# GNN with two residual-norm layers: one pick in every layer-0 step, 3.6 per layer-1 iteration, and the comparison numbers read from PSUM

## The reference, cut to what matters

```python
def _L0_gnn_ref(x, edge_index, edge_attr, W1, b1, W2, b2):
    src, dst = (edge_index[0], edge_index[1])
    tmp = jnp.concatenate([x[dst], x[src], edge_attr], axis=1)      # 48 + 48 + 32
    h = jax.nn.relu(tmp @ W1 + b1)                                  # 128
    msg = h @ W2 + b2                                               # 48
    return jax.ops.segment_sum(msg, dst, num_segments=N_NODES)
def _L1_gnn_ref(node_feat, edge_feat, src, dst, eps):
    m = jax.nn.relu(node_feat[src] + edge_feat)
    neigh = jax.ops.segment_sum(m, dst, num_segments=N_NODES)
    return (1.0 + eps[0]) * node_feat + neigh
x = _layernorm(x + _L0_gnn_ref(x, edge_index, edge_attr_32, W1, b1, W2, b2), axis=-1)
x = _layernorm(x + _L1_gnn_ref(x, edge_attr_48, src, dst, eps), axis=-1)
```

## Time and profile before

| | us |
|---|---|
| three runs | 4407.39, 4453.33, 4467.84; median 4453.33 |
| the profiled execution, its own time | 4415.78 |
| its span, first to last instruction | 4413.9 |
| TensorE's granted clock, mean over the span | 0.863 of full speed |
| busy: PE, PEld, VectorE, ScalarE, POOL | 3796.9, 2973.1, 2131.5, 664.9, 2860.8 |

### The profile page before, as it was taken

One profiled execution on the slowest core, in us unless ns is written; L12 is line 12 of the kernel. 1 busy time (PEld: TensorE's weight loads), 2 busy tenths in 40 slices (PEclk: granted clock), 3 DMA queues, 4 the chain that ended last, 5 costly groups with the idle time before them and its releaser, 6 DMA issues.

```text
span 4413.9 us, 56486 instructions
## 1 busy us (share of the span) xinstructions
PE 3796.9 (86%) x21170; PEld 2973.1 (67%) x21170; DVE 2131.5 (48%) x4283; ACT 664.9 (15%) x1275; POOL 2860.8 (65%) x2700
## 2 busy tenths in 40 slices
PE   4678888898999889899997898889689787897988
PEld 2556666676677667677766676668568576675777
DVE  1233333343333334334334576657468565674655
ACT  1212221122122122122221000000000000000111
POOL 6566666666666656656563677767678767676763
PEclk8678998898888888888887898889789998898888
DMA  4122222222222222222221122222122222221221
GB/s 99 28 34 32 33 34 32 32 35 32 34 32 35 32 32 34 32 32 34 35 35 33 41 49 48 46 43 53 39 46 55 45 45 44 43 52 39 50 48 41
DMA packets 407403, 178.33 MB, mean 40 GB/s; under 512 B 279173, under 2 KB 406291, under 8 KB 407027
## 3 DMA queue, kind: packets, MB, share of 16 engines
q0 software_dynamic: 86272, 66.43, 10.8%
q1 hardware_dynamic: 318738, 107.75, 10.7%
q10 hardware_dynamic: 2114, 0.49, 0.1%
HBM read 169.43 MB, written 5.00 MB: 40 GB/s over the span
## 4 chain that ended last, share of the span: by engine, by line
PE 65%; another core or an unknown queue 13%; issue 11%; POOL 5%; DVE 5%; DMA 0%; DVEq 0%; ACT 0%; POOLq 0%; SPq 0%
PE ps_h L830 12%; PE ps_t L830 12%; PE ps_early L830 11%; PE ps_m L740 8%; PE ps_h L791 7%; PE ps_as L732 6%; POOL edge L542 5%; PE ps_t L758 4%; PE ps_nodes L840 2%; PE ps_as L777 2%; DVE picked L1046 1%; DVE edge L957 1%; DVE at_place L1037 1%; DVE acc L971 1%
## 5 line engine op out<-in xcount | busy, mean ns | idle before, releaser
L542 POOL DMA_INDIRECT edge<-x,resid_sb x1438 | 1444.6, 1005 | 884.0 <-issue 405.3
L542 POOL DMA_INDIRECT edge<-x_dram,resid_sb x1258 | 1416.0, 1126 | 621.1 <-issue 381.8
L830 PE MATMUL ps_h<-x_parts,at_place 125*128 125x480 f32 x3080 | 772.7, 401 | 71.6 <-issue 64.1
L830 PE MATMUL ps_t<-x_parts,at_place 125*128 125x480 f32 x3040 | 771.5, 406 | 57.1 <-issue 54.8
L830 PE MATMUL ps_early<-x_parts,at_place 125*128 125x480 f32 x2520 | 706.7, 427 | 94.3 <-DVE edge L957 47.3
L830 PEld LDWEIGHTS ps_h<-x_parts,at_place 125*128 125x128 f32 x3080 | 600.4, 198 | 204.6 <-issue 104.3
L830 PEld LDWEIGHTS ps_t<-x_parts,at_place 125*128 125x128 f32 x3040 | 598.3, 201 | 185.8 <-issue 90.0
L830 PEld LDWEIGHTS ps_early<-x_parts,at_place 125*128 125x128 f32 x2520 | 498.1, 199 | 293.0 <-issue 170.5
L1037 DVE TENSOR_TENSOR at_place<-place_row,places_sb 125x1280 fp32r<-125x1280 f32 x432 | 640.1, 1482 | 1.4 <-DMA place_row<-rows_dram 1.2
L732 PE MATMUL ps_as<-edge,msg 128*48 128x48 f32 x6256 | 367.8, 222 | 219.1 <-issue 173.9
L732 PEld LDWEIGHTS ps_as<-edge,msg 128*48 128x48 f32 x6256 | 300.7, 132 | 330.0 <-issue 261.8
(11 more groups left out here) (63 smaller groups left out, 1769.0 us busy)
## 6 DMA issues: line engine op xcount, KB each, us to landing
e_sb<-e SPq DMA_DIRECT2D x196, 192.0 KB
place_row<-rows_dram SPq DMA_DIRECT2D x432, 62.5 KB
edge<-e SPq DMA_DIRECT2D x196, 128.0 KB
edge<-x,resid_sb POOLq DMA_INDIRECT x1438
edge<-x_dram,resid_sb POOLq DMA_INDIRECT x1258
x_win<-xT SPq DMA_DIRECT2D x391, 9.0 KB
acc<-xT SPq DMA_DIRECT2D x10, 234.4 KB
feats<-x SPq DMA_DIRECT2D x10, 234.4 KB
```

The costliest lines, as they stand in the source:

```text
L542: pool.indirect_dma_start(out=cols, out_offset=None, in_=rows_of, in_offset=bass.IndirectOffsetOnAxis(ap=index, axis=0)).then_inc(done, 16)
L830: last = nc.tensor.matmul(banks[q % len(banks)], lhsT=at_place[:, q % PLACED, c, :], rhs=x1_parts[:, c, part, :], start=(c == 0 and part = ...
```

## The change

- Layer 0: `plan_pairs` puts all ten units of one pick into every step from 19 to 187: 169 picks for 126.
- Layer 0, VectorE: `find_places` is called inside `offset_messages`, ahead of line 974 and behind the wait for the output layer, no longer after it. It is the same pick in the same step.
- Layer 1: the rates are 9 and 8 units in a step for 8 and 7: 345 picks for 306, or 3.6 in an iteration for 3.2 at first. A pick may be found half a step later relative to its first unit (1.5 for 1.9): 154 of the 345 are now found one step before their first unit is multiplied, where all were found two steps before.
- The numbers that `find_places` compares with are copied once to PSUM, behind `ps_m` in its bank, and read there (`ps_places` for `places_sb`). The bank's tensor is now named `ps_out`.

```diff
                 select = math.ceil(end - 0.38)
-                picks.append((select + 1, math.floor(begun - 1.9), select))
+                picks.append((select + 1, math.floor(begun - 1.5), select))
...
-    for s in range(first, last - 2, 4):
-        for begin, end in ((s, s), (s + 1, s + 1), (s + 2, s + 3)):
-            q, each = len(picks), CHUNKS // (end - begin + 1)
-            for step in range(begin, end + 1):
-                units[step] = [(q, (step - begin) * each + c) for c in range(each)]
-            picks.append((2 * (end + 2) + 1, begin - 1, end + 1))
+    for step in range(first, last):
+        units[step] = [(len(picks), c) for c in range(CHUNKS)]
+        picks.append((2 * (step + 2) + 1, step - 1, step + 1))
...
-PLAN, PRODUCTS = plan([(s, 10 if s < 0 else 8 if s < UNROLL * NORM_ITER else 7) for s in range(-AHEAD, GROUPS)], GROUPS - 1)
+PLAN, PRODUCTS = plan([(s, 10 if s < 0 else 9 if s < UNROLL * NORM_ITER else 8) for s in range(-AHEAD, GROUPS)], GROUPS - 1)
...
-        ps_m = pb("ps_m", [P, 2, TILES, D])
-        ps_iota = ps_m[:, 0, 0, 0:WIN]
+        ps_out = pb("ps_out", [P, 2 * TILES * D + CHUNKS])
+        ps_m = ps_out[:, 0:2 * TILES * D].rearrange("p (g t f) -> p g t f", g=2, t=TILES)
+        ps_iota = ps_out[:, 0:WIN]
+        ps_places = ps_out[0:NP, 2 * TILES * D:]
...
+            link(nc.vector.tensor_copy(ps_places, places_sb[:, :]))
...
                 if pair(p):
                     wait_for(dve, S0["msgp"], pair(p)[-1])
+                for q, (_, find, _) in enumerate(PLAN0):
+                    if find == p + 2:
+                        find_places(S0, q)
                 for g in pair(p):
                     add_b2(S0["msg"], g % UNROLL)
...
                 offset_messages(p - 2)
-                for q, (_, find, _) in enumerate(PLAN0):
-                    if find == p:
-                        find_places(S0, q)
...
                 nc.vector.tensor_tensor(at_place[:, q % PLACED, :, :], place_row[:, q % PLACED, :].unsqueeze(1).to_broadcast([NP, CHUNKS, P]),
-                                        places_sb[:, :].unsqueeze(2).to_broadcast([NP, CHUNKS, P]), ALU.is_equal).then_inc(S["places"], 1)
+                                        ps_places.unsqueeze(2).to_broadcast([NP, CHUNKS, P]), ALU.is_equal).then_inc(S["places"], 1)
```

## The result

The changed kernel takes **4578.73 us** (median of 4 runs, 4567.85 to 4580.75), the kernel before 4454.84 beside it: a ratio of 1.029, with a 95% interval of 1.022 to 1.037. It is slower by 124 us. The forecast was slower by 311. The sign is right, the size is two and a half times too large, and the time fell on a rival, "the slack takes in more" (4577), for which I had given 0.13. The profiled execution took 4580.46 us, 165 more than that of the kernel before, which was one of its fastest.

A forecast was written before the change was run, and what follows sets the result against it. TensorE, with slow stretches, was taken as the bound, POOL nearly as slow in layer 1. Layer 0 picks +164, layer 1 picks +197, gathers -50 made +311 on 4415.8, plus 37.5 for the median: 4764 us, range 4500 to 4870.

The forecast's parts named there:

- the slack takes in more: Rival: idle and waiting time absorbs added picks, +86 in layer 0, +38 in layer 1, 4577 us; chance 0.13.
- +197 for 780 matmuls: Layer 1: its 39 added picks add 780 matmuls at 0.252 us of TensorE busy time each, +197 us.
- -50 for the gathers: Layer 1: places in PSUM cut gathers from 1.126 to 0.95 us, saving 50 us of TensorE's waiting for POOL.
- I take 12.85, nearer to that: 168 x 12.85 = 2158.8: Layer 0: with 43 picks added, steps average 12.85 us, +162, and 2 for step 187: +164 us.
- a mean under 12.0: Layer 0 steps: a mean below 12.0 us would show the predicted mechanism wrong; 12.4 to 13.4 was expected.
- the other sign: TensorE's granted clock: a rise above 0.92 would show the mechanism wrong; near 0.87 was expected.
- in layer 0 a gather made faster is worth nothing: POOL waits there already: Layer 0: faster gathers save 0 us, as POOL already waits 345.7 us for transposes to free its ring.
- Edits at nothing: Both layers: VectorE's extra work, comparison before b2, later layer 1 comparisons, and PSUM copy with loads (at most 2 us) cost nothing.
- the bound of 20: Line 828: TensorE waiting over some 20 us for the comparison would show that its cover had failed.
- The clock gives it back: Rival, both layers: denser steps lose less to slow stretches, 4231 us; chance 0.07 faster by over 2%, 0.11 within 2%.
- The comparison late: Rival, layer 1: all 154 moved comparisons hold TensorE up by 1.48 us each, +228, 4992 us; chance 0.04.
- PSUM doesn't free the gathers: Rival, layer 1: gathers stay at 1.126 us and only the 50 us saving is lost, 4814 us; chance 0.06.

## Why the prediction was right, and where it was wrong

**Layer 1: right, in sum and in parts.** +197 for 780 matmuls and -50 for the gathers were to give +147; the window grew by 138. PE is busy 199 us more in it and idle 60 us less (291 before, 230 now). On that chip TensorE, with its slow stretches, took longer before the change and after than POOL's 1403 + 1247 x 0.30 = 1777 us (where the prediction sets POOL's 1524 beside 1998, that is the window's length and not POOL's need). So all that was added to it showed. That the 60 us are the gathers' isn't shown, since no kernel with the PSUM source alone ran on that chip. On the quiet chips the same two edits together shorten layer 1 (1804 to 1727), since POOL was ahead there. The term held for the chip whose trace it was read from, and for no other one here.

**Layer 0: this is the step that failed.** "I take 12.85, nearer to that: 168 x 12.85 = 2158.8", +164 with step 187; the steps came out at 11.95, +11, below even my low end of +86. The text had named a mean under 12.0 as the sign of a wrong mechanism, and the clock there, 0.92, stands at the other sign. The added work is +182 at full speed (84 x 2.16; the 10.34 of the earlier trace rows was at a clock of 0.97, and the fastest such step takes 10.04). What I held constant beside it, the loss over full speed, fell by 171, because 37 steps of 19 to 161 were slow where 69 had been.

The reading behind 12.85 was that a ten-unit step after another one averages 13.10 and one after a five-unit step 11.71, as if this were a property of such steps. The changed kernel refutes it: all its steps are alike, and by their place in the same pattern of four they average 14.34, 11.44, 11.26 and 10.77. These are averages over where slow steps happened to lie. The rival that I refused on "full steps show no idle time at all" was nearer for this layer, and even its +86 was too much.

Why the slow steps got fewer stays open. The quiet chips show a loss that falls too: the new table alone takes it from 182 to 97 us there (layer 0 of 1687 against 1505 at full speed, and 1783 against 1687), because POOL's limit drops out as soon as TensorE needs more than it. But that can't simply be carried over. On the quiet chip TensorE's idle time in layer 0 is 51 us of waits for gathered rows, and on the first chip its waits in this layer name no gather at all. Whether denser steps bring fewer slow ones, or one execution differs from the next by so much, I can't tell: one execution of each kernel was traced. It needs the kernel with layer 0's picks alone on a chip like the first.

**The sum, term by term.** Against the same profiled execution the forecast was +311 and the result +165. The forecast was 153 us too high in layer 0 and 9 in layer 1, and 16 too low outside the windows, which the sum had at nothing; that makes the 146 between them. A further 39 us of the miss in the median come from the base: 37.5 were added because the profiled execution of the kernel before was faster than its median, and for the changed kernel that distance is -2.

**Gathers: the mechanism right, the price wrong.** 0.95 us was forecast for layer 1 and 946 ns came; POOL's waits for line 1070 rose from 183 to 591, as said. But "in layer 0 a gather made faster is worth nothing: POOL waits there already" and the 50 for layer 1 are prices of one chip. Where TensorE runs undisturbed, the same faster gathers (with the move) are worth 101 us in layer 0 and 225 in layer 1. POOL's 345.7 us of waiting came with TensorE's slow stretches; where there are none it waits 24.9 us for the transposes in all of layer 0. The profile could have told this. At full speed a ten-unit and a five-unit step average 8.96 us, and POOL's 1240.94 us of busy time with 1225 gaps of 0.30 are 9.57 us a step. The four neighbours of the earlier trace rows showed the first number, and I never set the second beside it for layer 0, though I did for layer 1.

**Edits at nothing.** VectorE's additions and the copy stayed hidden: busy 888 and 1374 us of the two windows, no wait of TensorE for it but the 26 us for comparisons and 1.5 for b2. The 26 are over the bound of 20, so the cover was not whole; on the quiet chips the wait is gone (PE idle 2.4 us in the whole of layer 1). The move was not worth nothing but -36 there, the miss told above.

**The rivals.** "The slack takes in more" gave 4577 and the kernel takes 4579, but not by its parts: it put +86 in layer 0 and +38 in layer 1, and +11 and +138 came. That it names the right time is luck. "The clock gives it back": in part, and mostly in layer 0 (492 to 321, a third of the loss); in layer 1 the loss over full-speed pairs went from 460 to 2137 - 195 x 8.87 = 407, a ninth. "The comparison late" and "PSUM doesn't free the gathers" are refuted by the rows on waits and on gathers.

## What to carry to other kernels

When VectorE compares two long operands while GpSimd issues gathers and GpSimd is the bound, try one of them in PSUM: here, on the quiet chips, this was worth 8 to 9% together with the move. Then balance anew and only then: a table tuned for slow gathers has TensorE doing too much once they are fast, and the next step is not more of it. Before an engine's waits are called room, divide its work by the steps of the other engine at full speed; waits in a trace with slow stretches don't tell. And before an average over a class of steps is used as a price, look at the steps one by one: here the class averages were made by a few slow steps.

## What the runs showed of the hardware

- The same kernel takes 4407 to 4468 us in the first comparison and 3810 to 3848 on the three quiet chips, one core each. In the first, steps of 15 to 20 us come in 30 of 168, with idle time and stretches at a granted clock of 0.50; on the quiet chips no step reaches 15. A forecast in per cent from one chip's trace has to say on which kind of chip it holds.
- A granted clock of 0.50 also comes without idle time: in the last 25 steps of layer 0 of the changed kernel on a quiet chip PE is busy 338.68 of 338.68 us, and the clock averages 0.83.
- A gather that overlaps a comparison of 125x1280 elements with both sources in SBUF takes 1456 ns on average, with one source in PSUM 947; the comparison is no slower itself (1.48 us both ways). In layer 1 of the changed kernel, POOL is busy 1419.69 us with the SBUF source and 1144.14 with the PSUM one, 275 us for 345 comparisons, or 0.80 us each.
- The selection at line 1046, which reads one source from PSUM, does no such harm, though it takes 1.07 to 1.10 us: 100 gathers of layer 0 that have it alone beside them average 944 ns. The short addition at line 1070 (0.35 us, both sources in SBUF) costs little: 177 gathers of layer 1 beside it, and beside no comparison, average 984. Both are from the kernel with layer 1's picks alone.
- One execution of the changed kernel, of the 5 of its run on a quiet chip, took 16956.56 us; the others took 3844 to 3850. It is left out of the ratio, and nothing here explains it.
